# First pass loads two tiles in one transfer, issued in turns by SyncE and ScalarE

## The reference

```python
x = x + conv(group_norm(x), weights, bias)      # 8 groups of 2 channels
```

## Time and profile before

| | |
|---|---|
| median of 3 runs | 1967.86 us (1965.98 to 1968.54) |
| the profiled execution | 1968.76 us, its span 1966.8 us |
| first pass | from 3.7 us to about 681 us |
| second pass, steady part | from about 780 us to 1920 us |
| bytes | 551.75 MB read, 269.09 MB written, mean 418 GB/s over the span |
| TensorE, VectorE busy | 82% and 67% of the span |
| mean granted TensorE clock | 0.955 |

### The profile page before, as it was taken

One profiled execution on the slowest core, in us unless ns is written; L12 is line 12 of the kernel. 1 busy time (PEld: TensorE's weight loads), 2 busy tenths in 40 slices (PEclk: granted clock), 3 DMA queues, 4 the chain that ended last, 5 costly groups with the idle time before them and its releaser, 6 DMA issues.

```text
span 1966.8 us, 42532 instructions
## 1 busy us (share of the span) xinstructions
PE 1608.1 (82%) x19309; PEld 981.4 (50%) x19313; DVE 1308.9 (67%) x1261; ACT 81.8 (4%) x85; POOL 294.3 (15%) x669
## 2 busy tenths in 40 slices
PE   6888888888888899998877877877777777777773
PEld 6887888888888753443333333333333333333331
DVE  5988999999999826775555555545555555555552
ACT  0110111111101210000000000000000000000000
POOL 7444433333333400000000000000000000000000
PEclk9999999999999989999999989999999899999996
DMA  9999999999999966999999999999999999999998
GB/s 378 420 415 415 426 425 426 426 425 426 426 425 425 429 273 287 427 430 430 431 431 431 432 431 430 431 431 431 431 430 431 431 431 431 432 430 431 431 430 365
DMA packets 77806, 821.84 MB, mean 418 GB/s; under 512 B 10488, under 2 KB 10616, under 8 KB 11192
## 3 DMA queue, kind: packets, MB, share of 16 engines
q1 hardware_dynamic: 58056, 551.77, 66.5%
q10 hardware_dynamic: 19696, 269.40, 32.1%
HBM read 551.75 MB, written 269.09 MB: 417 GB/s over the span
## 4 chain that ended last, share of the span: by engine, by line
another core or an unknown queue 49%; DMA 31%; PE 9%; DVE 7%; SPq 2%; issue 0%; ACT 0%; POOL 0%; DVEq 0%
DMA early<-pairs 26%; PE ps L874 6%; DVE ring_own L608 6%; DMA out<-ring_own 2%; SPq L370 2%; DMA early<-strip_in 1%; DMA dia_in<-dia 1%; PE ps L775 1%; PE ps L882 0%; PE ps L881 0%; PE ps L801 0%; PE ps L802 0%; SPq L379 0%; PE ps L855 0%
## 5 line engine op out<-in xcount | busy, mean ns | idle before, releaser
L874 PE MATMUL ps<-ring_own,mixer 128*128 128x512 f32 x1252 | 589.3, 627 | 138.1 <-DMA ring_own<-strip_in 108.8
L750 PE MATMUL ps<-early 128*64 128x66 f32 x16896 | 580.3, 226 | 94.8 <-DMA early<-pairs 86.4
L608 DVE TENSOR_REDUCE ring_own<-early 128x32 f32<-128x2048 f32 x264 | 601.0, 2285 | 66.3 <-DMA early<-pairs 65.2
L750 PEld LDWEIGHTS ps<-early 128*64 128x64 f32 x16896 | 546.0, 139 | 129.0 <-DMA early<-pairs 104.3
L721 DVE SCALAR_TENSOR_TENSOR ring_own<-ps,row_sum,stage 128x512 f32<-128x512 f32 (+3 forms) x233 | 301.5, 1294 | 315.7 <-PE ps L874 315.7
L874 PEld LDWEIGHTS ps<-ring_own,mixer 128*128 128x128 f32 x1252 | 245.7, 201 | 482.0 <-issue 451.7
L874 PE MATMUL ps<-early,mixer 128*128 128x512 f32 x800 | 377.7, 629 | 90.3 <-DMA early<-strip_in 77.0
L721 DVE SCALAR_TENSOR_TENSOR early<-ps,row_sum,stage 128x1024 f32<-128x1024 f32 (+2 forms) x152 | 192.5, 1266 | 201.0 <-PE ps L874 201.0
L874 PEld LDWEIGHTS ps<-early,mixer 128*128 128x128 f32 x800 | 157.6, 201 | 309.9 <-issue 298.4
L433 POOL TENSOR_TENSOR gram_all<-gram_all,stage 128x512 f32<-128x512 f32 x132 | 166.9, 1287 | 0.0
L729 DVE SCALAR_TENSOR_TENSOR ring_own<-ps,row_sum,stage 128x488 f32<-128x488 f32 (+43 forms) x308 | 133.4, 475 | 0.0
(11 more groups left out here) (139 smaller groups left out, 130.5 us busy)
## 6 DMA issues: line engine op xcount, KB each, us to landing
early<-pairs SPq DMA_DIRECT2D x264, 1040.0 KB, 17.6
ring_own<-strip_in SPq DMA_DIRECT2D x78, 2048.0 KB, 23.3
out<-ring_own ACTq DMA_DIRECT2D x78, 2048.0 KB, 63.9
early<-strip_in SPq DMA_DIRECT2D x50, 2048.0 KB, 23.3
out<-early ACTq DMA_DIRECT2D x50, 2048.0 KB, 64.0
const<-const_f SPq DMA_DIRECT2D x1, 773.5 KB, 21.5
ring_own<-dia_pair SPq DMA_DIRECT2D x1, 640.0 KB, 21.3
ring_own<-half_in SPq DMA_DIRECT2D x1, 512.0 KB, 36.4
```

The source lines that it names most:

```text
L608: nc.vector.tensor_reduce(part_sum[:, t % sums], pairs_of(s), AX.XYZ, ALU.add).then_inc(summed, 1)
L750: last = mm(regions(parity)[lane:lane + WIDE, m // BANK_REGIONS, m % BANK_REGIONS], chunk(slot, k, False), chunk(slot, k, True), start=ope ...
L874: last = mm(ps[:, first + at // BANK, 0:piece], mixer[:, :, :].rearrange("p a m -> p (a m)"), buf[:, at:at + piece], start=True, stop=True)
```

## The change

Tiles `t` and `t + 1` (t even) are laid side by side in HBM and loaded by one transfer of 128 rows of 16640 bytes (2080 KB) into two neighbouring slots; a pair of slots shares one semaphore. I call such a transfer a double, by its first tile. SyncE issues doubles 0, 2, 4 and 6 at the start and, after that, those with `t % 4 == 0`; ScalarE issues those with `t % 4 == 2` behind its copy of a quad. A double is issued when both its slots are free. The computation is the same.

```diff
-    return v.reshape(len(tiles), BLK, VW), *as_units(z.reshape(len(strips(n)), BLK, n))
+    v = v.reshape(len(tiles) // 2, 2, BLK, VW).transpose(0, 2, 1, 3)
+    return np.ascontiguousarray(v).reshape(len(tiles) // 2, BLK, 2 * VW), *as_units(z.reshape(len(strips(n)), BLK, n))
...
-        v_in = [sem(f"v_in{s}") for s in range(V_SLOTS)]
+        v_in = [sem(f"v_in{s}") for s in range(V_SLOTS // 2)]
...
-            for t in range(len(tiles)):
+            for t in range(0, len(tiles), 2):
+                s = t % V_SLOTS
+                if t >= V_SLOTS and t % QUAD:
+                    continue
                 if t >= V_SLOTS:
-                    sp.wait_ge(gram_done, t - V_SLOTS + 1)
-                    sp.wait_ge(summed, t - V_SLOTS + 1)
-                sp.dma_start(vbuf[:, t % V_SLOTS], v[t]).then_inc(v_in[t % V_SLOTS], 16)
-                if t == V_SLOTS - 1:
+                    sp.wait_ge(gram_done, t - V_SLOTS + 2)
+                    sp.wait_ge(summed, t - V_SLOTS + 2)
+                sp.dma_start(early[:, s * VW:(s + 2) * VW], v[t // 2]).then_inc(v_in[s // 2], 16)
+                if t == V_SLOTS - 2:
                     sp.dma_start(const[:, :], const_f32).then_inc(const_in, 16)
...
                                      regions(q), ACT.Copy).then_inc(gram_staged, 1)
+                t = QUAD * (q + 2) + 2
+                if t < len(tiles):
+                    act.wait_ge(summed, t - V_SLOTS + 2)
+                    act.dma_start(early[:, (t % V_SLOTS) * VW:(t % V_SLOTS + 2) * VW], v[t // 2]).then_inc(
+                        v_in[t % V_SLOTS // 2], 16)
                 if q == 1:
                     act.wait_ge(dia_multiplied, 1)
...
-                dve.wait_ge(v_in[s], 16 * (t // V_SLOTS + 1))
+                dve.wait_ge(v_in[s // 2], 16 * (t // V_SLOTS + 1))
...
-                    pe.wait_ge(v_in[slot], 16 * (turn + 1))
+                    if slot % 2 == 0:
+                        pe.wait_ge(v_in[slot // 2], 16 * (turn + 1))
```

## The result

The changed kernel takes 1976.88 us (median of 5 runs, 1974.68 to 1979.45), the kernel before 1966.32 us in the runs beside it (5 runs, 1965.98 to 1968.54). The ratio is 1.0042, with a 95% interval from 1.0026 to 1.0058, so it is slower by 8 us, which is clear of noise. Timed again on another chip the ratio was 1.0058 (1.0045 to 1.0071). The profiled execution is the fastest of its five: 1974.68 us, span 1972.6.

What follows compares the result with a forecast made beforehand. It took the first pass as bound by DMA bytes over rate, the turn by a serial chain. Terms -8.5 + 4.8 + 3.4 = -0.3 us gave a median of 1967.6 us, range 1961.5 to 1975.5.

Steps and rivals of the forecast that it cites:

- second tile at the end: End of the first pass: two tiles, not one, stand between last landing and last copy; 2.3 us more.
- sharing at the end: End of the first pass: double 262 shares the DMA evenly with second-pass loads on SyncE's queue; 2.5 us more.
- term 1: First pass's tile loads: 16640-byte rows run at 431 GB/s, not 425.5; 8.5 us less, bounds 3.9 and 11.9.
- Term 3: Start: double 10 delays the tables, and TensorE restarts late; DMA holes of 2.5 and 0.9 us, 3.4 together, bounds 0 and 6.7.
- Term 2: End of the first pass: second tile behind the last landing plus shared DMA; 4.8 us more, bounds 4.5 and 7.2.
- B: Rival on the tile loads: larger rows bring nothing, rate stays 426 GB/s, costs remain; +8.2 us, 1976.1 us; chance 0.19.
- C: Rival on the slot ring: the two queues get out of step, DMA runs dry; 10 us, 1977.5 us; chance 0.06.
- A: Rival: rate rises 1.8% by the packets' time and the start has no hole; -7.1 us, 1960.8 us; chance 0.17.

Runs made afterwards that it cites:

- one_queue: Changed kernel, but SyncE issues all doubles in order and ScalarE none; 1967.84 us, ratio 0.9997 to the kernel before.
- start_by_sync: Changed kernel, but SyncE also issues doubles 10 and 14, ScalarE issuing from double 18 on; 1969.45 us, ratio 1.0007 to the kernel before.
- dia_first: Changed kernel, but ScalarE copies the diagonal product before it waits for tile 7 and issues double 14; 1972.82 us, ratio 1.0021 to the kernel before.
- last_by_sync: Changed kernel, but SyncE issues double 262, ahead of the second pass's loads; 1973.08 us, ratio 1.0028 to the kernel before.
- both_ends_by_sync: Changed kernel, but SyncE also issues doubles 10, 14 and 262, ScalarE 18 to 258 in turns with it; 1968.79 us, ratio 1.0008 to the kernel before.
- last_turn_unrolled: All doubles issued whole by SyncE, with TensorE's last turn of 8 tiles written out behind its loop; 1971.91 us, ratio 1.0019 to the kernel before.

## Why the prediction was wrong

Ledger of the last copy against before, in us:

| term | predicted | measured | from |
|---|---|---|---|
| 1, rate of larger rows | -8.5 (-11.9 to -3.9) | -2.9 | last landing, one_queue against before |
| 2, second tile at the end | +2.3 | +2.0 | 4.24 from landing to copy in one_queue, 2.25 before |
| 2, sharing at the end | +2.5 | +2.7 | start_by_sync against one_queue |
| 3, start | +3.4 (0 to 6.7) | +6.6 | changed kernel against start_by_sync |
| sum | -0.3 | +8.3 | changed kernel against before |

The measured terms are steps of one chain of kernels (before, one_queue, start_by_sync, changed), so their sum is the whole by construction and no test of them. Each is known to about half a microsecond.

The four places in the table were right, and the direction of each. **The step that failed is term 1**, and in it the choice of the row: "at 431 GB/s", from the second pass, "since in the changed kernel both queues are at work, as in the second pass, though there one of them writes". The number of queues turned out not to matter (one_queue), so that reason was empty; what the second pass has and the first has not is writes, though no run shows that they are what makes the 431. The other bound, 428 GB/s from the stretch that only reads large rows, was the rate that came, 428. And even it was not gained everywhere. My sum gave all 264 tiles the new rate; but from 100 to 200 us, with the small transfers of `step_m` and `step_mean` beside, the changed kernel moves 415 GB/s and the kernel before 416, and by 200 us one_queue and the kernel before have moved the same, 81.38 and 81.42 MB. So the gain came out below my lower bound of 3.9. That is 5.6 us of the 8.6 by which the sum was off.

**Term 3 was mis-sized,** 6.6 against 3.4 (6.1 by the changed kernel's other profile), near its upper bound of 6.7. The mechanism came as described, with tables at 36.6 (said: 36.3) and TensorE at 46.7 (46.6). Two sizes were off. For the first hole I let double 8 take its full 4.95 us from the tables' landing on, until 41.3. But a landing is seen later than the last byte flows (the first tile before landed 5.0 us after its issue, with 2.5 us of bytes), so part of double 8 was already through; the DMA fell silent near 39.5 us. Its GB/s in 40 slices from 30 to 90 us:

```profile
GB/s 455 388 458 388 477 388 111 0 177 355 488 377 277 422 421 311 255 422 410 399 322 366 432 399 399 388 410 310 355 388 455 388 444 399 466 410 422 455 422 433
```

Three slices of 1.5 us at 111, 0 and 177 are 3.5 us lost against a full rate of 428, not 2.5. For the second hole I counted one late double (0.9 us) and let both engines catch up at once; in fact the granted clock was 0.52 from 45 to 50 us, the case of the upper bound that I had named, and the DMA ran low several times until 80 us. dia_first gives 3.0 us back.

**Term 2** was right in size. The even split that I took holds to 682 us (56 to 45%) and not behind it, and moving 262 alone brings back only a part.

The rivals: B (no gain in rate, costs as said, 1976.1 us, 0.19) was nearest to the time. By its own test, less than 0.03 us a double saved, it came true over the whole pass (2.9 us over 132 doubles are 0.022) and not in the steady part (0.035 a double, 428 GB/s against 426). That its number fits is luck: the 2.9 us that did come and the 3.2 us that the start cost beyond my figure cancel. C didn't happen: there are no holes in the steady part. A is excluded. (The fit of the Trainium skill that the prediction quotes, 2.0 us plus the bytes over 436 GB/s, is given there, in DMA: Bandwidth & Descriptors, Anatomy of one DMA, for transfers that GpSimd issues; SyncE and ScalarE issue the loads here, and the sum took nothing from it.)

## What to carry to other kernels

A DMA-bound stage that is served by one queue has its order for free: what is needed first is issued first. The second queue here took a share at once, also from what was more urgent in the other, so it cost at the stage's start, where small tables are queued, and at its end, where the next stage's loads wait, and it brought no rate. When a rate is carried over from another stage, take the one that moves bytes in the same direction (here 428 for reads, 431 for reads and writes mixed), and when a wait is put into an engine's stream, ask what the next instruction on it releases.

## What the runs showed that I had not expected

**The turn between the passes differs by 10 us with TensorE's clock.** From the last copy to VectorE's first instruction of the second pass (L721 before, L723 or L730 in the others) it takes 52.3 us in start_by_sync, 52.5 in last_by_sync, 55.0 in the changed kernel and in both_ends_by_sync, 56.6 before and 61.8 in one_queue, with the same work. The mean granted clock from 682 to 745 us stands in the same order: 1.00, 1.00, 0.95, 0.95, 0.92 and 0.81. Windows of one_queue's profile:

```profile
700.00:705.00 5.00, 5.00 (x27) 4.31 (x27) 1.25 (x8) 1.06 (x3) 0.00 (x0) 0.50 1.02 429
730.00:735.00 5.00, 5.00 (x7) 2.02 (x6) 0.71 (x1) 1.39 (x3) 0.00 (x0) 0.51 0.00 0
```

and of start_by_sync's:

```profile
700.00:740.00 40.00, 36.39 (x179) 18.64 (x183) 17.12 (x77) 5.60 (x12) 0.00 (x0) 1.00 0.44 187
```

At half the clock (1.2 GHz of 2.4) the 8 matmuls of L858 took 6.81 us in one_queue, against 3.70 of the same step at full clock in the kernel before. Executions of one_queue take 1964.66 to 1976.95 us, and the profiled one, with these two falls of the clock, is one of the slowest (1975.33). This spread is as large as the effects studied here, which is why the last copy was read beside the times.

**Code written out in place of a loop** made TensorE stand twice, for 1.7 us each, with its data there (last_turn_unrolled). Its DMA view from 670 to 683 us has a line that one_queue's has not:

```profile
q8 instruction: 2, 0.03, 1.1%
```

Instructions were loaded in that stretch, then; that TensorE waited for them behind the full DMA fits, but no run tested it.
